# TensorE's loop body holds four steps in place of two, in a displaced convolution behind a group norm

## The reference

```
x = x + _L0_conv_ref(_gn(x), L0_conv_offset)
```

## Time and profile before

| | us |
|---|---|
| median of 3 runs | 1350.67 |
| lowest and highest | 1348.41, 1353.38 |
| the profiled execution's own time | 1354.66 |
| its span, first to last instruction | 1352.8 |
| TensorE busy (share of the span) | 1213.8 (90%) |
| VectorE busy | 991.2 (73%) |
| ScalarE busy | 942.3 (70%) |
| GpSimd busy | 274.3 (20%) |
| mean granted TensorE clock | 0.992 |

### The profile page before, as it was taken

How to read it: one execution, slowest core, us unless ns; L and a number is a source line. 1 busy time by engine, 2 the same in 40 slices (tenths; PEclk the granted TensorE clock), 3 DMA queues, 4 the chain that set the end, 5 groups by cost and what they waited for, 6 DMA issues and landing times.

```text
span 1352.8 us, 110317 instructions
## 1 busy us (share of the span) xinstructions
PE 1213.8 (90%) x49408; PEld 1142.0 (84%) x49408; DVE 991.2 (73%) x1530; ACT 942.3 (70%) x851; POOL 274.3 (20%) x646
## 2 busy tenths in 40 slices
PE   0888999999999999999999999999999999999897
PEld 0788888888898888888888888888888888888787
DVE  7667677777777777777777777777777777777543
ACT  3566776767777677776767777677777767777464
POOL 3211222122121211212121222212212122121010
PEclk9989999999999999999999999999999999999899
DMA  9589899999999999999999999999999999999745
GB/s 313 160 265 314 271 309 311 314 314 315 318 301 316 314 316 308 318 307 320 308 313 316 313 311 320 301 324 310 310 320 306 311 313 318 318 311 309 234 164 187
DMA packets 409771, 403.14 MB, mean 298 GB/s; under 512 B 16528, under 2 KB 409744, under 8 KB 409744
## 3 DMA queue, kind: packets, MB, share of 16 engines
q1 hardware_dynamic: 204944, 201.41, 48.2%
q10 hardware_dynamic: 204800, 201.36, 44.0%
HBM read 201.38 MB, written 201.33 MB: 298 GB/s over the span
## 4 chain that ended last, share of the span: by engine, by line
PE 89%; issue 7%; DVE 2%; ACT 0%; POOL 0%; ACTq 0%; POOLq 0%; DVEq 0%
PE yp L572 56%; PE xp L591 29%; PE xp L557 4%; DVE stats L395 1%; ACT y L507 0%; DVE xin L414 0%; ACT norm L498 0%; ACT next_ay L487 0%; POOL grid_i L200 0%; ACTq L523 0%; DVE t_msk L372 0%; DVE ay L382 0%; DVE tap_sum L358 0%; DVE tap_inv L361 0%; DVE sub L338 0%
## 5 line engine op out<-in xcount | busy, mean ns | idle before, releaser
L572 PE MATMUL yp<-ay,norm 32*128 32x128 f32 x24576 | 766.4, 276 | 66.8 <-ACT y L507 44.8
L572 PEld LDWEIGHTS yp<-ay,norm 32*128 32x128 f32 x24576 | 718.1, 188 | 89.9 <-issue 82.4
L507 ACT ACTIVATE y<-yp 128x1536 f32<-128x1536 f32 x256 | 371.5, 1451 | 310.5 <-PE yp L572 310.3
L498 ACT ACTIVATE norm<-xin,bias,rstd 128x768 f32<-128x768 f32 x512 | 496.9, 1018 | 53.4 <-issue 43.3
L395 DVE BATCH_NORM_STATS2 stats<-xin 128x6 f32<-128x512 f32 x768 | 508.4, 692 | 0.0
L591 PE MATMUL xp<-ax,y 64*64 64x64 f32 x24576 | 421.0, 221 | 9.6 <-issue 8.8
L591 PEld LDWEIGHTS xp<-ax,y 64*64 64x64 f32 x24576 | 384.8, 135 | 41.5 <-issue 10.9
L411 DVE TENSOR_TENSOR xin<-xp,xin 128x512 f32<-128x512 f32 x256 | 176.9, 691 | 321.6 <-PE xp L591 321.6
L414 DVE TENSOR_TENSOR xin<-xp,xin 128x1024 f32<-128x1024 f32 x256 | 309.4, 1208 | 12.2 <-PE xp L591 12.2
L241 POOL TENSOR_TENSOR stats<-stats 128x12 f32<-128x12 f32 x128 | 27.0, 211 | 986.6 <-DVE stats L395 980.0
L258 POOL TENSOR_TENSOR rstd<-var,mhalf 128x8 f32<-128x8 f32 x64 | 104.9, 1639 | 5.0
(11 more groups left out here) (52 smaller groups left out, 105.9 us busy)
## 6 DMA issues: line engine op xcount, KB each, us to landing
xin<-in_x_dram SPq DMA_DIRECT2D x512, 384.0 KB, 5.4
out_dram<-xin ACTq DMA_DIRECT2D x512, 384.0 KB, 4.2
off<-in_L_conv_offset_dram SPq DMA_DIRECT2D x1, 48.0 KB, 3.2
```

The lines of the kernel that those rows point to most:

```text
L498: nc.scalar.activation(norm[:, s % 2, :, cols].rearrange("p r (q w) -> p q r w", w=HW), xin[:, s, QG * g:QG * (g + 1)].rearrange("p q (r w ...
L507: nc.scalar.activation(y[:, v].rearrange("p k r a m -> p a (k r) m"), yp[:, :, 0:POS * P].rearrange("p a (n m) -> p a n m", m=32), ACT.Cop ...
L572: last = nc.tensor.matmul(yp[:, a, P * k:P * (k + 1)], norm[rows, v, r, P * k:P * (k + 1)], ay[rows, k, r, :], start=(r == 0), stop=(r == ...
```

## The change

TensorE's loops take a body of four steps, made of two calls of `two_steps`, in place of two steps. The index of the statistics' slot is `2 * u + w`, with `u` the register of the loop and `w` a constant; the matmul reads the same data. In superblock 0, the first eight steps are now written out (two calls of `four_steps` outside a loop), where the first two were written out and a loop of 3 followed. The main loop's innermost loop runs 2 times in place of 4. The order of the work on TensorE, its waits and all other engines stay as they are.

```
-            def two_steps(c, i, j, first=False, more=True):
+            def two_steps(c, i, u, w, first=False, more=True):
...
+            def four_steps(c, h, u, first=False, more=True):
+                two_steps(c, 4 * h + 2 * u, u, 0, first, more)
+                two_steps(c, 4 * h + 2 * u + 1, u, 1, more=more)
...
-            two_steps(0, 0, 0, first=True)
-            with pe.Fori(1, 4) as j:
-                two_steps(0, j, j)
-            with pe.Fori(0, 4) as j:
-                two_steps(0, j + 4, j)
+            four_steps(0, 0, 0, first=True)
+            four_steps(0, 0, 1)
+            with pe.Fori(0, 2) as u:
+                four_steps(0, 1, u)
             with pe.Fori(1, NSUPER - 1) as c:
                 with pe.Fori(0, 2) as h:
-                    with pe.Fori(0, 4) as j:
-                        two_steps(c, 4 * h + j, j)
-            with pe.Fori(0, 4) as j:
-                two_steps(NSUPER - 1, j, j)
-            with pe.Fori(0, 4) as j:
-                two_steps(NSUPER - 1, j + 4, j, more=False)
+                    with pe.Fori(0, 2) as u:
+                        four_steps(c, h, u)
+            with pe.Fori(0, 2) as u:
+                four_steps(NSUPER - 1, 0, u)
+            with pe.Fori(0, 2) as u:
+                four_steps(NSUPER - 1, 1, u, more=False)
```

More of the change, by code:

```diff
@@ L549, in _, with sum_stats @@
         def _(pe):
-            def sum_stats(pair, j, t=None):
+            def sum_stats(pair, u, w, t=None):
                 pe.wait_ge(stats_ready, pair + 1)
@@ L557, in sum_stats @@
                 nc.tensor.matmul(xp[:, 3, 1, 0:2 * GROUPS * 9], ones[:, :],
-                                 stats[:, bass.ds(j, 1)].rearrange("p v t g s -> p (v t g s)"),
+                                 stats[:].rearrange("p (u w) t g s -> p u w (t g s)", w=2)[:, bass.ds(u, 1), w]
+                                 .rearrange("p u f -> p (u f)"),
                                  start=True, stop=True).then_inc(stat_summed, 1)
@@ L603, in two_steps @@
                 if more:
-                    sum_stats(pair, j, None if first else t)
+                    sum_stats(pair, u, w, None if first else t)
                 y_products(t + 1, 1)
                 x_products(t, 0, pair, c + 1)
+            def four_steps(c, h, u, first=False, more=True):
+                two_steps(c, 4 * h + 2 * u, u, 0, first, more)
+                two_steps(c, 4 * h + 2 * u + 1, u, 1, more=more)
             pe.wait_ge(filled, FILLS)
-            for j in range(4):
-                sum_stats(j, j)
-            two_steps(0, 0, 0, first=True)
-            with pe.Fori(1, 4) as j:
-                two_steps(0, j, j)
-            with pe.Fori(0, 4) as j:
-                two_steps(0, j + 4, j)
+            for u in range(2):
+                for w in range(2):
+                    sum_stats(2 * u + w, u, w)
+            four_steps(0, 0, 0, first=True)
+            four_steps(0, 0, 1)
+            with pe.Fori(0, 2) as u:
+                four_steps(0, 1, u)
             with pe.Fori(1, NSUPER - 1) as c:
                 with pe.Fori(0, 2) as h:
-                    with pe.Fori(0, 4) as j:
-                        two_steps(c, 4 * h + j, j)
-            with pe.Fori(0, 4) as j:
-                two_steps(NSUPER - 1, j, j)
-            with pe.Fori(0, 4) as j:
-                two_steps(NSUPER - 1, j + 4, j, more=False)
+                    with pe.Fori(0, 2) as u:
[4 more added lines that the diff above has]
+                four_steps(NSUPER - 1, 1, u, more=False)
             x_products(TOTAL - 1, 1)
```

## The result

The changed kernel takes 2037.8 us (median of 4 runs, 2015.23 to 2063.52) against 1351.68 before; the ratio is 1.494, 95% interval 1.487 to 1.501. The ratio is that of the two faster runs, 2015 and 2023 us (the other two took 2053 and 2064, and whether something disturbed them or one or two passes more were slow is not shown), and the profiled execution is the one of 2023.07. My likeliest case said 1372. The time lies inside my wide range of 1345 to 2050 and inside rival A's 1840 to 2230, to which I had given 0.23.

What follows compares the result with a forecast made beforehand. TensorE's work and its gaps were taken to bound the kernel. If the longer body stayed in instruction memory: 1354.66 - 10 (edges) + 30 (added code) = 1375 us profiled, so 1372 us; wide range 1345 to 2050.

Steps and rivals of the forecast that it cites:

- rival A: Main loop's code is fetched anew, all of it, on each of 56 passes: 1840 to 2230 us; chance 0.23.
- the resident body: The longer main-loop body stays in TensorE's instruction memory, new code fetched once: 1355 to 1400 us, likeliest 1372; chance 0.47.
- the two that refetch: Rival A and Rival B, in which main-loop passes fetch code again; chances 0.23 and 0.16.
- Edges that go: 66 loop edges, now inside bodies, lose register add and branch: 0.15 us each, 10 us gained, ends 0 and 22.
- What is late next: Without the branch, ACT's copy of y decides when the y product behind a former loop edge starts.
- Register work: Some ten more register operations in four steps, costed at nothing; at kept edges 6 us at the most.
- Code that is added: Six new copies of `two_steps`, each fetched once, 18 or 19 more packets: 30 us lost, ends 6 and 46.
- The clock behind the stops: After a stop for code, TensorE runs at a lower granted clock; included in first-pass prices of 5.2 to 7.7 us.
- Rival B: Only the loop head's packet is missed at the main loop's back edge, 3 to 6 us a pass: 1540 to 1710; chance 0.16.
- Rival C: Faster: straight code streams in under the matmuls, added copies cost next to nothing: 1329 to 1341 us; chance 0.06.
- D: No change to be measured: copies at about 2 us each pay for the edges, 1350 us; chance 0.08.
- The rule of the Trainium skill: TensorE's instruction memory: 8 blocks, a FIFO; a body touching 7 fits with one fetched ahead, one touching 8 doesn't.

Runs made afterwards that it cites:

- the run with 12 instructions: The changed kernel with 12 instructions that only add to an unused semaphore put ahead of the main loop: 1371.74 us, ratio 1.013 to the kernel before.
- the run with the main loop alone: Kernel before with four steps in the main loop's body only, other loops at two, 48 one-slot instructions ahead of it: 1354.2 us, ratio 1.0011.

## Why the prediction was wrong

The step that failed is the premise of the sum, "if the longer body still stays in the instruction memory". I had the mechanism, and a count of the code that put the main loop's head about 5 instructions ahead of a packet's edge (compiled, it is 6) and so the body in 8 packets. I held the capacity for unshown and the count for uncertain by just that much, and gave the resident body 0.47 against 0.39 for the two that refetch. What I had put against refetching, that nothing was fetched twice before, says nothing here: the old body touches 4 packets. The runs show the capacity from both sides. A pass without a packet over a body of 8, as from 324.3 to 344.4 us, means that 8 are held. A loop nest in 7 with an eighth fetched ahead never fetches again (1371.74 us). A body or nest in 8, with the ninth ahead, fetches 225 to 306 packets again in its 56 passes.

Point by point:

*The sum for the resident body.* It was 1372 us, and the run with 12 instructions ahead, in which the body does stay, took 1371.74. The sum was right in size; the case wasn't. That the two agree to 0.3 us is luck: that run is 18.4 us above its own kernel before (1353.34), 2.0 of them for the 12 instructions, so the change cost 16.4 where I had 30 - 10 = 20.

*Edges that go.* I took 0.15 us for each. Where the main loop's edges were, the wait went from 0.33 to 0.20 us, so 0.13. In the run with 12 instructions a superblock takes 79.9 us in place of 80.5. These are its window and that of the kernel before:

```profile
212.60:292.50 79.90, 74.88 (x3096) 70.57 (x3091) 61.23 (x94) 58.73 (x54) 16.94 (x39) 1.00 0.96 315
```

```profile
612.00:692.50 80.50, 75.03 (x3104) 70.63 (x3094) 61.34 (x94) 58.89 (x54) 16.92 (x39) 1.00 0.96 313
```

Fourteen superblocks save some 7 to 8 us; with superblocks 0 and 15, 66 edges at 0.13 are 8.6, where I had 10.

*What is late next.* ACT's copy of y, as I said: 334.95 has [0.20 <-ACT y L507].

*Register work.* The first register instruction of the body takes 170 ns in place of 147; 64 x 0.023 us is 1.5 us at the most: next to nothing, as costed.

*Code that is added.* I had 30 us for six copies, 5 each. The run with 12 instructions has a span of 1370.4, 17.6 us above before; with 8.6 us gained at edges and 2.0 us for the 12 instructions, the copies cost about 24, 4.0 each; the run with the main loop alone says 4.9. My term was a little large. Its form was right: 37 packets where I had said 36 or 37.

*The clock behind the stops.* I counted it only within the prices of first passes. In the changed kernel it is a third of the loss: 220 us of busy time of 668.

*Rival A.* Its condition was the right one, and its price, 470 to 860 us, holds the 668 measured, but it is made differently. I let all 56 passes refetch at 8 to 15 us. The trace has 34 that do, at 18.3 us in the pair of windows above, with two stops at the head (7.36 and 1.92) where I had two of 3 us. Against the span of the run with 12 instructions, 1370.4, the 651 us more are 19.1 for each of the 34. That more than a third of the passes go free I had not seen: behind a refetching pass the memory holds exactly the body's 8, and the ninth is not always asked for within the 40 to 50 instructions that the last packet has ahead of the back edge. Why it is asked for in some passes and not in others is not shown.

*Rival B* is out: its 1540 to 1710 us were missed and nine packets, not two, come in a pass. *Rival C and D* are out with the run of 12: the stops of new code are real, and even where the body fits, the kernel with its six added copies is slower than before by 1.3%.

*The rule of the Trainium skill.* The Trainium skill, "Runtime: NRT & Kernel Launch", section "Instruction fetch mechanics", says that TensorE's instruction memory is a FIFO of 128 KiB in 16 KiB blocks, and that a taken branch to a target outside the window, which it puts at 2 pages, forces a fetch before execution goes on. The traces agree with the 8 blocks of 256 instructions, and with the fetch: the branch lasts 5.4 to 8.5 us where the head's packet is gone. That the memory drops what was loaded first, and not what was used longest ago, no run was made to tell. The 2 pages do not hold for TensorE here, nor does the remark on 2 lines beside it: the pass from 324.3 to 344.4 us ran over 8 packets and fetched none.

What would have decided it: to weigh the count as the best number there was. Its error had to be 5 of some 3900 (3 x 781 + 1582) for the other case, and I had no row that spoke for such an error.

## What to carry to other kernels

Look at the instruction queue of a profile before a loop's body grows: how many packets in all, and whether any come while the loop runs. In every run here without a hint, a loop nest on TensorE that lay, with all its outer heads, in 7 packets of 256 instructions was fetched once, and one that touched 8 was fetched again and again, since one more is fetched ahead of its end. Whether a nest of some 1590 instructions lies in 7 hangs on its place, and so on any code ahead of it. And code is not free where it is run once: 4.0 to 4.9 us for each copy of some 790 instructions here, and 0.15 us for each instruction put in only to move the loop. Folding six copies of a body into three and the nest into one loop gained 2.7%, where the longer body lost 49% at the place where it fell and the same code lost 1.3% 12 instructions further on.

## What the runs showed that I had not expected

At a back edge to a packet that is gone TensorE stood idle for 7.4 us at 293.96 (up to 8.6 elsewhere), more than twice the longest stop of a first pass, 3.07: the branch itself lasts that long. In the trace of the changed kernel the innermost loop's branch has these durations, in ns (min/median/max), where it had 76/208/226:

```profile
L623 PEldq COMPARE_BRANCH  x56: 76/160/8490, 168.1 to 1921.2; - x56
```

In all 34 refetching passes two packets start within 0.01 to 1.9 us of each other behind the branch's start, by the account above the ninth and the head's, while the DMA engines have a share of 0.63. In 24 of these passes the branch is that of the innermost loop, and in the 11 of them with the two packets at least 0.65 us apart the branch ends 1.35 to 1.53 us behind the landing of the later one, and 2.9 to 3.2 us behind the earlier. At the single packets behind it, in the passes that begin at 293.96 and 351.99, the stopped matmuls go on 1.2 to 1.5 us behind the landing. So the branch ends as if it waited for the later of the two, which lengthens the stop. Which of the two is the head's, and what a lone packet would have cost, is not shown.
